# Two causal attention stages: set-up taken chunk by chunk, and the latent stage run chunk-outer

## The reference, cut to what matters

```python
# rope attention: 16 heads of 8
q, k, v = split((x @ W_qkv).heads, 3); q = rope(q); k = rope(k)
o = softmax(where(causal, q @ k.T / sqrt(8), -inf)) @ v
out = o.reshape(B, T, 128) @ W_out.T
# latent attention: 8 query heads of 128 in 2 groups, one key/value latent of 32 per group
k = (x @ wk_down) @ wk_up; v = (x @ wv_down) @ wv_up
o = softmax(where(causal, q @ k.T / sqrt(128), min)) @ v
out = o.reshape(B, T, 1024) @ wo
```

## Time and profile before

| | |
|---|---|
| median of three runs | 1938.54 us |
| span of the profiled execution | 1933.1 us |
| PE busy | 1601.7 us (83%) |
| DVE busy | 1180.5 us (61%) |
| POOL busy | 818.4 us (42%) |
| ACT busy | 786.5 us (41%) |
| rope stage, first projection to last output | about 371 to 932 us |
| latent stage, first projection to last output | about 1362 to 1847 us |
| packets of SP's DMA queue (q1) | 27906, 29.29 MB |
| packets of ACT's DMA queue (q10) | 3520, 6.29 MB |

### The profile page before, as it was taken

The page is one execution under the profiler, slowest core; times in us unless marked ns, Lnnn a source line. Parts: engine busy times, 40 slices in busy tenths (PEclk is TensorE's granted clock), DMA queues, the critical chain, the costliest instruction groups (busy, mean ns, idle before and its releaser), DMA issues.

```text
span 1933.1 us, 25832 instructions
## 1 busy us (share of the span) xinstructions
PE 1601.7 (83%) x8863; PEld 807.4 (42%) x8863; DVE 1180.5 (61%) x2315; ACT 786.5 (41%) x1031; POOL 818.4 (42%) x987
## 2 busy tenths in 40 slices
PE   4766699758999899999799789989545898988779
PEld 2222466412333333332466567766212333333256
DVE  5887633578788787883333333342355878897951
ACT  2222233343565565667333344444212343334433
POOL 2224646464554635455463644000001577456900
PEclk8788699867999999999799999979656898889979
DMA  4000000151000303000000000000143000000000
GB/s 139 1 0 0 1 1 0 59 121 29 2 2 12 41 3 51 2 2 1 1 1 0 0 1 0 0 1 0 49 117 96 1 1 1 1 1 1 1 1 22
DMA packets 31585, 36.86 MB, mean 19 GB/s; under 512 B 8606, under 2 KB 24703, under 8 KB 31362
## 3 DMA queue, kind: packets, MB, share of 16 engines
q1 hardware_dynamic: 27906, 29.29, 6.4%
q10 hardware_dynamic: 3520, 6.29, 1.6%
q0 software_dynamic: 64, 0.00, 0.0%
HBM read 26.10 MB, written 8.91 MB: 18 GB/s over the span
## 4 chain that ended last, share of the span: by engine, by line
PE 61%; DVE 16%; DMA 7%; SPq 3%; issue 2%; ACT 2%; ACTq 0%; DVEq 0%
PE PS L943 9%; PE PS L1355 9%; PE PS L931 9%; PE PS L1304 8%; PE PS L1374 8%; DVE sb_latent_acc L1462 3%; DMA sb_rope_K<-rope_parts 3%; PE PS L1723 3%; PE PS L1741 3%; SPq L1629 2%; DVE sb_latent_mp L1538 2%; DMA latent_parts<-sb_latent_parts 2%; DVE sb_rope_mp L1538 2%; DVE sb_latent_rec L1568 1%; PE PS L1735 1%
## 5 line engine op out<-in xcount | busy, mean ns | idle before, releaser
L1538 DVE TENSOR_REDUCE sb_rope_mp<-PS 128x1 f32<-128x512 f32 (+3 forms) x560 | 345.0, 669 | 76.5 <-PE PS L1308 36.9
L1418 ACT ACTIVATE sb_rope_PT<-PS 128x1024 f32<-128x1024 f32 (+3 forms) x320 | 273.3, 895 | 223.0 <-PE PS L1359 121.7
L1462 POOL TENSOR_TENSOR sb_latent_acc<-sb_latent_acc,sb_latent_PT 128x1536 f32<-128x1536 f32 (+3 forms) x72 | 223.2, 3101 | 72.4 <-ACT sb_latent_PT L1418 68.8
L1418 ACT ACTIVATE sb_latent_PT<-PS 128x1024 f32<-128x1024 f32 (+3 forms) x160 | 140.2, 895 | 243.3 <-PE PS L1359 80.9
L995 DVE SCALAR_TENSOR_TENSOR sb_X<-PS,sb_gates,sb_X 128x128 f32 (+1 forms) x320 | 90.1, 344 | 241.3 <-PE PS L943 241.2
L1304 PE MATMUL PS<-sb_rope_K,sb_rope_Q 96*128 96x512 bf16 (+3 forms) x640 | 211.7, 371 | 30.2 <-ACT sb_rope_V L1399 18.3
L1538 DVE TENSOR_REDUCE sb_latent_mp<-PS 128x1 f32<-128x512 f32 (+3 forms) x280 | 174.3, 666 | 46.2 <-PE PS L1304 32.5
L576 POOL TENSOR_SCALAR sb_pbelow<-sb_pa,sb_ptrial 128x512 f32<-128x512 f32 x124 | 197.0, 1599 | 6.4
L583 POOL TENSOR_TENSOR sb_pbelow<-sb_pbelow 128x1024 f32<-128x1024 f32 (+1 forms) x248 | 181.7, 733 | 19.6
L931 PE MATMUL PS<-sb_HT,sb_w 128*128 (+1 forms) x384 | 182.3, 612 | 3.6 <-DVE sb_seed L514 1.9
L1355 PE MATMUL PS<-sb_rope_Q,sb_rope_K 99*128 99x512 bf16 (+3 forms) x640 | 179.4, 352 | 1.4 <-ACT sb_rope_PT L1418 0.9
(11 more groups left out here) (291 smaller groups left out, 2438.7 us busy)
## 6 DMA issues: line engine op xcount, KB each, us to landing
latent_parts<-sb_latent_parts SPq DMA_DIRECT2D x36, 128.0 KB
sb_rope_Q<-rope_parts SPq DMA_DIRECT2D x9, 384.0 KB
rope_parts<-sb_rope_parts SPq DMA_DIRECT2D x24, 128.0 KB, 2.4
sb_rope_tab<-in_rotation SPq DMA_DIRECT2D x1, 2048.0 KB, 8.6
sb_rope_K<-rope_parts SPq DMA_DIRECT2D x6, 256.0 KB
sb_latent_Q<-latent_parts ACTq DMA_DIRECT2D x2, 768.0 KB
sb_latent_Q<-latent_parts SPq DMA_DIRECT2D x1, 1536.0 KB, 19.1
sb_rope_Q<-rope_parts ACTq DMA_DIRECT2D x6, 192.0 KB
```

The lines of the kernel that those rows point to most:

```text
L1418: s.activation(self.PT[:, u % 2, 2 * p:2 * p + 2, q0:CH], k.PS[:, 2 * p:2 * p + 2, q0:CH], ACT.Exp, scale=self.scale).then_inc(self.exps[p ...
L1462: eng.tensor_tensor(acc, acc, new, ALU.add).then_inc(self.added[who], 1)
L1538: v.tensor_reduce(self.mp[:, n % 2, kc, heads[0]:heads[-1] + 1, i], k.PS[:, bank, 0:len(heads) * w].rearrange("p (h k) -> p h k", h=len(he ...
```

## The change

`parts` gets two buffers, and a chunk's roundings wait for the stores of two chunks ago. Stores of parts 0 and 1 count on one semaphore, those of part 2 on another; in the latent stage parts 0 and 1 of a source go in one DMA, and the scratch is (3 sources, 3 parts, 128 rows, T), so that a store's rows are the 128 partitions on both sides (24 store DMAs for 36). All stack loads move to SP. They go by `load_early(n)`: chunk n of the stage's order over 512 columns, 8 DMAs in the rope stage (quad 0's four chunks) and 12 in the latent stage (all eight chunks, since blocks are cut to one part each; 96 load DMAs for 24). SP stores chunk c, then issues the loads of place n = c in the order; the latent stage's other four are issued behind the turns of places 1 to 4. The maximum rows of the first chunk are sent from ACT's queue. The rope stage's quad g + 1 is now loaded at the turn of chunk 1 of quad g, behind its rows and after a wait that all units ahead of quad g are weighed. The latent stage's order becomes c outside and g inside, and `PT` and `acc` lie in buffers of stages that are over. The plan's rule is as it was; with the new order it puts 27 items up front in the latent stage where it put 46 (in the rope stage 56 as before). ACT writes the constants of chunk c + 1 ahead of the values of chunk c.

```diff
+        self.index = dict((gc, n) for n, gc in enumerate(order))
...
+        self.parts = sb("parts", [P, 2, ns, 3, CH], BF16)
+        if self.homes:
+            self.PT = self.homes[0:2]
...
         if kind == "max":
             _, g, c, i, kc, heads = item
-            if g == 0:
-                pe.wait_ge(self.first[2 * c // NC], self.first0 + 16 * self.stack_dmas)
+            n = self.chunk(g, c)
+            if n < self.early:
+                pe.wait_ge(self.first[n % 2], self.first_done(n))
...
             pe.wait_ge(self.max_rows[n % 2], 16 * 4 * (n // 2 + 1))
+            if n < self.early and self.NP > 1:
+                pe.wait_ge(self.second[n % 2], self.second_done(n))
...
+        self.write_constants(s, 0)
+        for c in range(NC):
+            if c >= 2:
+                s.wait_ge(self.stored_lo, self.lo_done(c - 2))
+                s.wait_ge(self.stored_hi, self.hi_done(c - 2))
...
+            if c + 1 < NC:
+                self.write_constants(s, c + 1)
+            s.wait_ge(self.filled, self.use + 1)
+            s.wait_ge(self.vproj, self.use * NC + c + 1)
...
+        self.max_row_dmas(s, *self.order[0])
...
+    def store_parts(self, sp, c):
+        ns, cols = len(self.sources), slice(c * CH, (c + 1) * CH)
+        if c:
+            sp.wait_ge(self.stored_lo, self.lo_done(c - 1))
+            sp.wait_ge(self.stored_hi, self.hi_done(c - 1))
+        for i in range(ns):
+            sp.wait_ge(self.rounded, self.rounded0 + (2 * c + 1) * ns + i + 1)
+            if self.rotate:
+                for part in range(2):
+                    sp.dma_start(self.scratch[i, :, part * 8:(part + 1) * 8, cols],
+                                 self.parts[:, c % 2, i, part, :]).then_inc(self.stored_lo, 16)
+            else:
+                sp.dma_start(self.scratch[i, 0:2, :, cols].rearrange("q p t -> p q t"),
+                             self.parts[:, c % 2, i, 0:2, :]).then_inc(self.stored_lo, 16)
+        for i in range(ns):
+            sp.wait_ge(self.split, c * ns + i + 1)
+            out = self.scratch[i, :, 16:24, cols] if self.rotate else self.scratch[i, 2, :, cols]
+            sp.dma_start(out, self.parts[:, c % 2, i, 2, :]).then_inc(self.stored_hi, 16)
+
+    def load_early(self, sp, n):
+        g, c = self.order[n]
+        cols = slice(c * CH, (c + 1) * CH)
+        sp.wait_ge(self.constants, self.constants0 + (c + 1) * self.n_constants // NC)
+        sp.wait_ge(self.stored_lo, self.lo_done(c))
+        if self.rotate:
+            sp.wait_ge(self.stored_hi, self.hi_done(c))
+        if n >= 2:
+            sp.wait_ge(self.first[n % 2], self.first_done(n - 2))
+        self.load_stacks(sp, g, cols, [0], self.first[n % 2])
+        if self.NP > 1:
+            sp.wait_ge(self.stored_hi, self.hi_done(c))
...
+            self.load_stacks(sp, g, cols, range(1, self.NP), self.second[n % 2])
...
     def sync(self, sp):
...
+        loaded = 0
         for c in range(NC):
-        for sem in self.stored:
-            sp.wait_ge(sem, 16 * self.split_dmas * NC)
-        sp.wait_ge(self.constants, self.constants0 + self.n_constants)
-        self.load_stacks(sp, 1, slice(0, T), self.stacked[1])
+            self.store_parts(sp, c)
+            if loaded < min(self.early, NC):
+                self.load_early(sp, loaded)
+                loaded += 1
...
         for u, item in self.plan:
             if item[0] == "turn":
                 _, g, c = item
-                if c == NC - 1 and 2 <= g + 1 < self.NQ:
-                    sp.wait_ge(self.weighted, g * len(self.units))
-                    self.load_stacks(sp, g + 1, slice(0, T), self.stacked[(g + 1) % 2])
                 n = self.chunk(g, c)
+                if n:
+                    self.max_row_dmas(sp, g, c)
+                    if loaded < self.early:
+                        self.load_early(sp, loaded)
+                        loaded += 1
+                if c == 1 and self.early < len(self.order) and g + 1 < self.NQ:
+                    if g:
+                        sp.wait_ge(self.weighted, self.starts[self.index[g, 0]])
+                    self.load_stacks(sp, g + 1, slice(0, T), range(self.NP), self.stacked[(g + 1) % 2])
...
+                            [(g, c) for g in range(4) for c in range(NC)], NC)
...
+                            [(g, c) for c in range(NC) for g in range(2)], 2 * NC,
+                            homes=[k.w0[:, :, :].rearrange("p (j e) h -> p j (e h)", j=4),
...
-    d["latent_parts"] = nc.dram_tensor("latent_parts", (3, 4, 3 * 32, T), BF16).ap()
+    d["latent_parts"] = nc.dram_tensor("latent_parts", (3, 3, P, T), BF16).ap()
```

More of the change, by code:

```diff
@@ L154, in __init__ @@
     def __init__(self, k):
-        self.first = [k.sem(f"first{h}") for h in range(2)]
+        self.first = [k.sem(f"first{b}") for b in range(2)]
+        self.second = [k.sem(f"second{b}") for b in range(2)]
+        self.stored_lo = k.sem("stored_lo")
+        self.stored_hi = k.sem("stored_hi")
         self.filled = k.sem("filled")
@@ L1142, in __init__ @@
         self.ready = s("ready")
-        self.units = [(c, kj) for c in range(NC) for kj in range((c + 1) * TPC)]
+        self.starts = [0]
+        for _, c in order:
+            self.starts.append(self.starts[-1] + (c + 1) * TPC)
+        self.total = self.starts[-1]
         self.plan = self.make_plan()
@@ L1182, in make_plan @@
     def make_plan(self):
-        n = len(self.units)
-        total = self.NQ * n
+        total = self.total
         items, due = [], []
-        for g in range(self.NQ):
-            for c in range(NC):
-                items += self.chunk_maxima(g, c)
-                due.append((g * n + self.units.index((c, 0)), len(items)))
+        for n, (g, c) in enumerate(self.order):
+            items += self.chunk_maxima(g, c)
+            due.append((self.starts[n], len(items)))
         def wanted(u):
@@ L1200, in make_plan @@
         steps = [[] for _ in range(total + 7)]
[L1201 removed]
+        turn_at = dict((d, self.order[i]) for i, (u, d) in enumerate(due))
         up_front, pending = [], []
@@ L1215, in make_plan @@
         relays = []
-        for g in range(self.NQ):
-            for c in range(NC):
-                end = g * n + self.units.index((c, (c + 1) * TPC - 1))
-                if self.summed:
-                    steps[end + 2].append(("sum", g, c))
-                    steps[end + 3].append(("out", g, c))
-                else:
-                    relays.append((end + 2, "sums", g, c))
-                    relays.append((end + 4, "reciprocals", g, c))
-                    steps[end + 6].append(("sum", g, c))
-                    steps[end + 7].append(("out", g, c))
+        for n, (g, c) in enumerate(self.order):
+            end = self.starts[n + 1] - 1
+            if self.summed:
+                steps[end + 2].append(("sum", g, c))
+                steps[end + 3].append(("out", g, c))
+            else:
+                relays.append((end + 2, "sums", g, c))
+                relays.append((end + 4, "reciprocals", g, c))
+                steps[end + 6].append(("sum", g, c))
+                steps[end + 7].append(("out", g, c))
         plan = [(None, it) for it in up_front]
@@ L1246, in unit @@
     def unit(self, u):
-        g, i = divmod(u, len(self.units))
-        c, kj = self.units[i]
+        n = max(i for i in range(len(self.order)) if self.starts[i] <= u)
+        g, c = self.order[n]
+        kj = u - self.starts[n]
         q0 = max(0, kj - c * TPC) * P
@@ L1337, in first_unit @@
     def first_unit(self, n):
-        g, c = divmod(n, NC)
-        return g * len(self.units) + self.units.index((c, 0))
+        return self.starts[n]
     def pe_scores(self, pe, u, p):
@@ L1443, in gpsimd @@
             return
-        for u in range(self.NQ * len(self.units)):
+        for u in range(self.total):
             self.add_weights(g, u, 0, slice(0, 3))
@@ L1451, in add_weights @@
         if kj == 0 and n:
-            b, uses = self.ring_bank(self.ring_items().index(("sum", (n - 1) // NC, (n - 1) % NC)))
+            b, uses = self.ring_bank(self.ring_items().index(("sum",) + self.order[n - 1]))
             eng.wait_ge(self.ring_full[b], uses + 1)
@@ new lines, in first_done, with second_done, lo_done, hi_done @@
+    def first_done(self, n):
+        return self.first0 + 16 * self.loads_of([0]) * (n // 2 + 1)
+    def second_done(self, n):
+        return self.second0 + 16 * self.loads_of(range(1, self.NP)) * (n // 2 + 1)
+    def lo_done(self, c):
+        return self.lo0 + 16 * len(self.sources) * (2 if self.rotate else 1) * (c + 1)
+    def hi_done(self, c):
+        return self.hi0 + 16 * len(self.sources) * (c + 1)
+    def max_row_dmas(self, eng, g, c):
+        n = self.chunk(g, c)
+        b, uses = self.ring_bank(self.turned_at(g, c))
+        eng.wait_ge(self.ring_free[b], uses + 1)
+        for j in range(4):
+            eng.dma_start(self.Q[self.rows:self.rows + 3, g % 2, j, 0, c * CH:(c + 1) * CH],
```

(1 more changed line is left out.)

141 lines of the change are left out of this document (72 added, 69 removed).

## The result

| | before | after |
|---|---|---|
| median of the runs, us | 1938.54 (1936.07 to 1945.7) | 1891.4 (1890.95 to 1893.11) |
| ratio, 95% interval | 1 | 0.9747, 0.9718 to 0.9776 |
| profiled span, us | 1933.1 | 1888.7 |
| rope stage: first projection to first item, to first exponential | 45.0, 87.4 | 35.6, 72.4 |
| rope stage: first `sums` DMA to last | 453.7 | 496.5 |

The kernel is 2.5% faster. The forecast was 1896.5 with a range from 1860 to 1915. On the profiled executions the change brought 44.4 us, and on the medians 47.1, where 42 were forecast.

A forecast was written before the change was run, and what follows sets the result against it. TensorE (PE) held 61% of the chain of waits; the change could only work on the DMA and queue shares, some 10% of 1933 us. -56 - 16.5 - 3.3 + 34 = -42 took the median from 1938.5 to 1896.5; range 1860 to 1915.

The forecast's parts named there:

- Part A: Latent stores over 16 engines and two buffers: PE's first item 36 us sooner, at 1391.5 instead of 1427.6.
- Part B: Latent front, first item to first exponential: 20 us instead of 48.2, a gain of 28 us.
- Part C: Latent stage: 19 items now lie between units and cost 8 us there.
- my two ends: Latent items moved between units: 0.29 us or 0.58 us an item, 5.5 to 11 us in all.
- Part D: Rope set-up: first item 11 us sooner, first scores from 457.0 to 440.5, -16.5 us.
- Part E: Rope loads of quads 2 and 3: PE's waits go, -3.3; `sums` relay held behind eight loads at two boundaries, +34.
- clock term: Rope quad boundaries: low granted clock after PE's idling costs up to 7.4 us, taken as 3 at each.
- Rival 1: Rope quad boundaries: the relay's packets slip between the loads, sum -76, 1862 us; chance 0.20.
- Rival 2: Latent stores don't spread, a chunk's stay at 13 us: -18, 1920 us; chance 0.05.
- Rival 3: Latent set-up: SP's issues become the bound, at 2 us each +48, 1986 us; decides from 1.35 us; chance 0.05.

The follow-up runs named there:

- e4b: Changed kernel with the latent scratch as before, (3, 4, 96, T), so store groups of 32 rows do not join, nine stores a chunk, two buffers: 1907.3 us.
- e9: Changed kernel with the latent stage's second buffer unused, roundings waiting for the stores of chunk c-1: 1893.9 us.
- e3: Changed kernel with the latent order turned back to quad-outer: 1897.0 us.
- e5: Kernel before with only the loads of rope quads 2 and 3 moved forward to the turn of chunk 1, behind its rows: 1972.1 us.
- e13: Kernel before with only GpSimd's two largest adds each issued as four instructions of a quarter: 1935.1 us, ratio 0.9965.
- e4: Changed kernel with latent stores described as 4 groups of 32 rows, which join in the new scratch, nine DMAs a chunk: 1888.3 us.
- e1: Changed kernel with the whole loads of rope quads 2 and 3 put back to the turn of chunk 3: 1866.1 us.
- e11: e1 with GpSimd's two largest adds each issued as four instructions of a quarter (short adds): 1850.6 us.
- e8: Changed kernel with the loads of rope quads 2 and 3 issued from ScalarE's queue, the sums DMA staying on SyncE's: 1893.3 us.
- e12: e2 plus the short adds of e11 (GpSimd's two largest adds in quarters): 1846.1 us.
- e2: Changed kernel with every rope quad loaded in four pieces by chunk, each issued behind the return of a reciprocal: 1859.8 us.

## Why the prediction was right, point by point

**Part A (first item 36 us sooner): right in mechanism, 5 us too small.** It was 41.3. I had let 4 us of waiting for chunk 1's stores stand; 2.6 were left. The larger error is the 5 us of projection and rounding that were to come out from under the waits: it was 44.9 - 2.6 - 41.3 = 1.0. The mean granted clock from first projection to first item was 0.58 before and is 0.86 now, which I hadn't counted; that it explains the 4 us isn't shown. e4b gives 18 us of the 41.3 to the shape, e9 9 us to the second buffer. Each was taken out alone, with the other in place, so the remaining 14 are what the two save together and whatever else came with them; no run separates these. The four engines' worth did carry: in e4b the stores moved at 3.7. But the price showed as SP's issue time, not as landing time.

**Part B (28 us from first item to first exponential): right.** It was 48.2 before and 20.2 after. e3 gives 11 us to the order. The other 17 fit the loads per chunk: DVE's 17.2 us of idling for the second half's stacks is gone, in e3 too. No run takes those loads back alone. A place's twelve small loads were out in 5.5 us (1396.51 to 1402.0), and one landed in 2.7. The rule on small transfers of the Trainium skill, "DMA: Bandwidth & Descriptors", section Bandwidth, would have taken 18 us from the latent stage's gain, 56 to 38, and made the sum -24. The trace disagrees with it here: the latent stage gained 68.7 us.

**Part C (8 us back for the moved items): open.** Between the two profiles it was 0.6, and 0.4 between e3 and the kernel after. But this stretch scatters by as much as the term: e5 and e13 have the latent stage of the kernel before and took 366.6 and 366.5 us where that took 370.1, and the kernels with the stage of the change took 369.5 (e4) to 376.8 (e1 and e11). So these pairs bear out neither my 8 nor nothing, and my two ends weren't tested.

**Part D (rope set-up -16.5): right**, -15.0 at the first exponential, -9.4 at the first item where I had 11.

**Part E (relay held, +34): right.** The stretch from the `sums` of chunk 3 to the next `sums` grew from 9.3 to 22.0 us behind quad 0 and from 9.4 to 22.4 behind quad 1, the one after by 3.4 and 3.6: 32.7 in all. That is 2 x (14 + 3) = 34 with its clock term. By medians e5 gives 31. DVE stood 15.3 and 15.5 us where I had 16.7, PE 14.9 and 15.2 where I had 14. The -3.3 for PE's wait for K can't be told from the scatter.

**What the sum hid.** Profile against profile, the latent stage gained 68.7 and not 56, and the rope stage's part from the first exponential on lost 42 and not 31. Two misses of about 12 us cancelled, and that the total came out within 5 us of the forecast is partly luck. The one in the latent stage is parts A and C, and so in part the scatter named there. The one in the rope stage, 10 us beyond the held relays, was no term of mine. Part of it is pauses at the chunks' turns: in the profile after, small operations of DVE took 2.08 us at 794.55 and 2.28 us at 855.89, and PE stood 4.0 and 3.9 us in front of these two turns. That the rest is of the same kind, or plain scatter as among the six kernels with this stage, is argued and not shown.

**The range.** By its own terms the rope stage's upper end is -16.5 - 3.3 + 2 x 21.5 = +23, not the +27 of the prediction, so the range of the forecast ends at 1914 or so instead of 1918. Nothing else hangs on it.

**The rivals.** Rival 1 (the relay is not held) fell. In the one queue its packets moved last, and from a queue of its own (e8) they did slip between, and it was late all the same. Rival 2 (the stores don't spread) fell with the 2.6 us left of ACT's waits; e4b is what it would have looked like, 1907 where I had 1920. Rival 3 fell: issues stayed at 0.4 to 0.6 us, far from the 1.35 from which it decided.

**A version that beats both.** The loads in pieces behind the reciprocals and the short adds (e12) took 1846.1 us, 0.9511 of the kernel before, 45 us under the change. Most of that is the place of the loads of quads 2 and 3: without the short adds e2 is 32 us under it, and e1 25.

## What to carry to other kernels

Moving a large load earlier is not free because its data are ready: look at which small DMA is issued next, and at who waits for it. Here 23 us of load packets ahead of a relay of 132 small ones cost 16 us each time; cutting the load into pieces that fit between two relays gave all of it back between `sums` and `sums`, and another queue gave nothing back. And take a forecast apart by stage even where its sum is right, since two errors had cancelled here.

## What was not expected of the hardware

- A DMA of 132 packets on another queue than the loads still took 22 us: none of its packets moved for 8 us, then they moved among those of the loads (e8).
- A store of 4 groups of 32 rows is as quick as one of 128 rows where the groups join in DRAM (2.2 us to landing, issue 0.45), and takes 1.42 us of SyncE's issue time (median of a chunk's last three) where they don't (e4, e4b).
- DVE operations of 0.17 us took 2.31 and 1.12 us beside GpSimd's adds of 2.36 and 1.27 (e1), and the pause of 4 us that followed on PE left the granted clock at about 0.5 for some 5 us.
- The stages between rope and latent, which no edit to the two stages touched, took 433 to 434 us from the last `sums` DMA to the first latent projection in the profiles of the kernel after, e1, e4b, e8 to e12, 437 in those of the kernel before and e13, 440 in e4's, and 447 in those of e2, e3 and e5, with granted clocks of 0.92 and 0.93 in two stretches of e2 (913 to 1066 and 1066 to 1255) where e1 had 0.95 and 0.97 in the same work. What sets it stayed open. The latent stage behind its first exponential likewise took 370.7 us in the profile after and 376 to 377 in those of e1, e2, e11 and e12, and that stayed open too. The traces give a lead: DVE's 48 adds of 128x512 to the sums of the weights, beside GpSimd's, took 1.3 us each in the profile after and 1.73 to 1.87 in these four. It isn't the whole answer, since they took 1.75 to 1.89 in e3 and e9 as well, whose stretches were 370.2 and 370.7.
